# The four expert rows of a token are summed by one strided reduction on VectorE instead of two additions on POOL

## What is computed

```python
topk_idx, topk_weight = _gate(x, gate_w, e_bias)     # 4 of 16 experts for each token
inter = jax.nn.silu(g) * u                            # per expert
expert_out = jnp.einsum('eti,ehi->eth', inter, down_proj)
sel = expert_out[topk_idx, jnp.arange(T)[:, None]]
y = jnp.einsum('tkh,tk->th', sel, topk_weight)        # the sum over the four rows of a token
...
return y + shared_out
...
x = _layernorm(x + _L0_ffn_ref(x, ...), axis=-1)
```

## Time and profile before

| | us |
|---|---|
| median of three runs | 789.55 |
| the three runs | 783.31, 789.55, 789.67 |
| the profiled execution | 784.78 |
| its span (first to last instruction) | 782.1 |

### The profile page before, as it was taken

How to read it: one execution, slowest core, us unless ns; L and a number is a source line. 1 busy time by engine, 2 the same in 40 slices (tenths; PEclk the granted TensorE clock), 3 DMA queues, 4 the chain that set the end, 5 groups by cost and what they waited for, 6 DMA issues and landing times.

```text
span 782.1 us, 24288 instructions
## 1 busy us (share of the span) xinstructions
PE 731.6 (94%) x9544; PEld 508.8 (65%) x9544; DVE 546.0 (70%) x1549; ACT 433.7 (55%) x880; POOL 273.8 (35%) x320
## 2 busy tenths in 40 slices
PE   5979999999999999999999999998799999999983
PEld 2547666756676776567667756776677787775643
DVE  8477755369546686865758599448989558943887
ACT  4867776264756534567565354753146766664331
POOL 7222112011232110625311054230265255556872
PEclk9999999999999999999999999999989999999997
DMA  8335676424000000311300041043686225424461
GB/s 281 141 95 155 189 149 162 126 54 127 2 3 2 3 2 19 120 41 45 95 2 3 2 156 55 9 165 136 210 272 188 64 92 171 147 82 161 141 208 56
DMA packets 55181, 80.78 MB, mean 103 GB/s; under 512 B 12576, under 2 KB 43424, under 8 KB 54560
## 3 DMA queue, kind: packets, MB, share of 16 engines
q1 hardware_dynamic: 48416, 62.71, 26.3%
q0 software_dynamic: 5376, 15.47, 5.1%
q10 hardware_dynamic: 1280, 1.05, 0.5%
HBM read 42.65 MB, written 33.41 MB: 97 GB/s over the span
## 4 chain that ended last, share of the span: by engine, by line
PE 65%; DVE 25%; issue 3%; ACT 2%; DMA 2%; SPq 1%; POOL 1%; ACTq 0%; DVEq 0%
PE ps L1657 28%; PE ps L1663 14%; PE ps L1755 7%; PE ps L1736 3%; PE ps L1880 3%; DVE xmax L1519 3%; PE ps L1771 3%; DVE st L1328 2%; DVE rows L1345 2%; PE ps L1799 1%; PE ps L1772 1%; DVE root_a L1337 1%; SPq L766 1%; PE ps L1944 1%; DVE attn_mem L1485 1%
## 5 line engine op out<-in xcount | busy, mean ns | idle before, releaser
L968 POOL TENSOR_TENSOR qk<-square,qk 128x512 f16<-128x512 f32 x64 | 75.8, 1186 | 258.9 <-ACT qk L1060 258.8
L1657 PE MATMUL ps<-x_split,w_qkv 128*128 128x512 f16 x384 | 93.8, 382 | 2.9 <-DVE qk L1481 1.9
L1663 PEld LDWEIGHTS ps<-attn_mem 128*64 128x64 f32 x1920 | 78.6, 138 | 24.0 <-issue 21.3
L1663 PE MATMUL ps<-attn_mem 128*64 128x65 f32 x1920 | 93.3, 226 | 0.3 <-issue 0.2
L990 POOL DMA_INDIRECT rows_out<-attn_mem,dest x64 | 62.5, 977 | 41.3 <-ACT attn_mem L1161 26.7
L983 POOL DMA_INDIRECT rows_in<-rows,slot_i x48 | 47.5, 989 | 73.3 <-DVE slot_i L1418 61.2
L1481 DVE SCALAR_TENSOR_TENSOR qk<-ps,qk 128x512 f16<-128x512 f32 x64 | 43.8, 684 | 41.8 <-ACT square L1057 41.6
L1063 ACT ACTIVATE attn_mem<-ps 128x512 f32<-128x512 f32 x64 | 37.7, 595 | 62.1 <-PE ps L1736 62.0
L1101 ACT ACTIVATE prob<-ps 128x512 f32<-128x512 f32 x96 | 52.9, 603 | 21.5 <-PE ps L1663 12.2
L1657 PEld LDWEIGHTS ps<-x_split,w_qkv 128*128 128x128 f16 x384 | 37.1, 98 | 37.7 <-issue 3.9
L1657 PE MATMUL ps<-attn_mem,w_qkv 128*128 128x128 f16 x512 | 55.8, 223 | 3.2 <-DVE attn_mem L1585 2.5
(11 more groups left out here) (307 smaller groups left out, 1872.7 us busy)
## 6 DMA issues: line engine op xcount, KB each, us to landing
attn_mem<-rows_in SPq DMA_DIRECT2D x64, 144.0 KB, 2.4
late_mem<-ffn_w SPq DMA_DIRECT2D x17, 384.0 KB, 3.6
rows_in<-zero_row SPq DMA_DIRECT2D x32, 144.0 KB, 4.8
up_split<-late_mem SPq DMA_DIRECT2D x16, 256.0 KB, 2.8
x_stage<-xT SPq DMA_DIRECT2D x4, 512.0 KB, 5.7
down_split<-late_mem SPq DMA_DIRECT2D x16, 128.0 KB, 2.8
rows<-x SPq DMA_DIRECT2D x4, 512.0 KB, 6.9
xq<-late_mem SPq DMA_DIRECT2D x32, 64.0 KB
```

The lines of the kernel that those rows point to most:

```text
L968: pool.tensor_tensor(parts[:, 3, :], square[:, n % 2, :], parts[:, 2, :], ALU.subtract).then_inc(p_sql.sem, 1)
L1657: ins = pe.matmul(dst, lhs(i), rhs(j), start=first and n == 0, stop=last and n == 2)
L1663: ins = pe.matmul(dst[at:at + COLS, :], lhs[:, at:at + COLS], rhs, start=start, stop=stop)
```

## The change

POOL's branch `combine` is removed, and with it the signal `paired`. DVE waits for the landed rows itself, sums the four rows with one `tensor_reduce` whose input is read with the four rows innermost (a stride of 256 floats, 1,024 bytes), into `row_sum`, the first 256 floats of `x_mem`, waits for that by a new signal `joined`, and folds `row_sum` into the sums. The order of all lists, the fetches and the three buffers stay. The sum of the four rows is taken in another order.

```diff
+        row_sum = x_mem[:, 0:D]
...
-        folded = signal("folded"); paired = signal("paired", 2)
+        folded = signal("folded"); joined = signal("joined")
...
-                elif kind == "combine":
-                    i = NT * b + n
-                    four = yg[i % YG]
-                    pool.wait_ge(*yg_loaded[i % YG](i // YG + 1, 0))
-                    pool.tensor_tensor(four[:, 0:2, :], four[:, 0:2, :], four[:, 2:4, :], ALU.add).then_inc(paired.sem, 1)
-                    pool.wait_ge(*paired(i, 1))
-                    pool.tensor_tensor(four[:, 0, :], four[:, 0, :], four[:, 1, :], ALU.add).then_inc(paired.sem, 1)
...
-                    dve.wait_ge(*paired(i + 1, 0))
-                    four = yg[i % YG]
-                    dve.tensor_tensor(total[:, n, :], four[:, 0, :], total[:, n, :], ALU.add).then_inc(folded.sem, 1)
+                    dve.wait_ge(*yg_loaded[i % YG](i // YG + 1, 0))
+                    dve.tensor_reduce(row_sum[:, :], yg[i % YG].rearrange("p k d -> p d k"), AX.X, ALU.add
+                                      ).then_inc(joined.sem, 1)
+                    dve.wait_ge(*joined(i, 1))
+                    dve.tensor_tensor(total[:, n, :], row_sum[:, :], total[:, n, :], ALU.add).then_inc(folded.sem, 1)
                     dve.wait_ge(*folded(0, i + 1))
                     statistics(n, total)
```

## The result

The changed kernel takes **794.89 us** (median of 10 runs, 792.93 to 799.62); the kernel before takes 784.24 (10 runs, 781.27 to 789.67). The ratio of the means is **1.0126, with a 95% interval of 1.0097 to 1.0156**: 9.9 us slower (10.7 between the medians). The forecast was 791, from 3.8 us of loss on a base of 786.8. The base was 2.6 above the median of before, since those runs spread over 8 us and do not sit on two levels, and the loss was too small by a factor of 2.6. The range, 783 to 800, holds the time, but not by the sum: 3.8 on the measured 784.24 would be 788.0. The too high base made up for 2.6 of the missing us, and the upper end of the range was there for rival B. The profiled execution took 792.93, its span is 790.0.

What follows compares the result with a forecast made beforehand. DVE's chain from 733.92 to 771.09 was taken to bound the changed part: reductions add 11.3 us, POOL waits give 5.1 back, some 2 of other waits are filled, so 3.8 more on 786.8 gives 791, range 783 to 800.

Steps and rivals of the forecast that it cites:

- rival B: DVE's new reduction: the stride halves its speed, 2.29 us instead of 1.22, 13 us lost in all; chance 0.22.
- What bounds the stage: From expert 9's gating (733.92) to the first `total` step (771.09), DVE's own chain of 37.17 us sets the time.
- The price of POOL's additions: DVE after 733: of 9.2 us of waits beside POOL, 5.5 belong to `combine`'s two additions and go.
- The reduction at 1.22 us: DVE's new four-row sum: 1024 strided elements take 1.22 us, as a contiguous reduction does, 1.25 with the step.
- nine reductions add 11.3: The nine new reductions on DVE's chain after 733 lengthen it by 11.3 us.
- New collisions: Folds right behind a `dense weigh` meet POOL's `dense keep` and end some 0.6 us late; waits for POOL still about 4.1.
- Rival C: Folds miss POOL's `dense keep`, which falls under the reduction; all 4.1 us of waits go, 0 to -1 us; chance 0.13.
- The stretch before 733 costs 0: Three combines before 733 add 3.8 us to DVE, which fit in its 4.3 us of slack.
- The moved wait: DVE itself waits for fetched rows, landing 3.4 to 7.6 us after issue; 8 us or more are available, so no cost.
- rival D: Fetches land late, so DVE waits for rows once or twice, 1 to 3 us each: 788 to 793; chance 0.05.
- The chances: Whole kernel: 0.03 for faster by over 1%, 0.72 for within 1%, 0.25 for slower by over 1%.

Runs made afterwards that it cites:

- act_order: Changed kernel with ACT's silu of expert 14 put ahead of block 1's `norm3` copies; timed ratio to the kernel before 1.0131.
- contig: Changed kernel with the reduction adding four neighbouring floats, read contiguously (another sum); timed ratio to the kernel before 1.0038.
- nosum: Changed kernel without the sum of four rows, the fold adding row 0 alone; timed ratio to the kernel before 0.9953.
- merge: Kernel before, sums still on POOL, with the inverse roots of blocks 1 and 2 taken as one; timed ratio to it 0.9954.
- tree: Changed kernel with the strided reduction replaced by two contiguous additions on DVE; timed ratio to the kernel before 1.0105.
- poolback: Changed kernel with POOL's two additions put back on scratch data that no result uses; timed ratio to the kernel before 1.0196.
- strides2: Changed kernel with single DVE reductions and additions of several sizes and strides appended at its end; 16 floats took 164 ns contiguous, 179 at 16 bytes.

## Why the prediction was right or wrong

- **What bounds the stage** (DVE's list from gating 9 to the totals): right. act_order moved PE's stop without a change of time; contig, nosum and merge came within 0.3 us of their replays. The replay is too low where more operations meet POOL's: tree came out 1.5 us above it, poolback 2.2.
- **The price of POOL's additions** (5.5 of 9.2 us of waits, and some coming back): right. nosum gives -4.0 for -3.8, poolback shows the waits with nobody waiting for a result.
- **The reduction at 1.22 us: the step that failed.** The term "nine reductions add 11.3" was 9 x 1.97 = 17.7, the 1.93 us with the step behind it. The length itself was read rightly: the row of 1,220 ns was of f16 and had 64 outputs, and contig's reduction of f32 to 256 takes 1.21 as well. What failed was the stride. I took 1.22 since 171 ns for 16 elements at 16 bytes stood beside 170 for 16 contiguous ones. But these were two different reductions, to four outputs and to one. In strides2, where only the stride differs, 16 floats take 164 and 179 ns: the penalty is there, 15 ns, and the comparison was off by 6 already. At 512 floats it is 0.69 against 1.06. A row with 16 elements could not bear a term of 1024.
- **Rival B** (chance 0.22) was the mechanism that came, at 1.63 times per element instead of twice, so 8 to 10 us instead of 13. Its line of decision, a reduction of 1.8 us for a loss of 1%, fits: 1.93 gave 1.26%. Of the prediction's signs of being wrong two came together, a reduction above 1.8 us (B) and all folds at 0.42 (C). The section "Specifications (TRN2)" of the Trainium skill's page "SBUF — State Buffer" says that each crossing to a new 16-byte line pays unless a line is hit twice; the step between 8 and 16 bytes agrees with it. That groups of two pay nothing at 2,048 bytes is not in that sentence.
- **New collisions** (4.1 us of waits left): wrong in the changed kernel, by the same term: at 1.93 the fold comes just as POOL's subtraction ends. In contig they are there, 1.01 for 0.42, six of them for the five forecast. (The working has `dense keep` hold until 2.57; 1.43 + 1.16 is 2.59, which changes nothing.) Rival C had this mechanism; it came about through a longer reduction and not through an earlier subtraction, and so it made the loss smaller but gave no gain.
- **The stretch before 733 costs 0:** wrong by 1.5 us, by the same term again. A combine takes 3.00 us there (723.02 to 726.02) instead of 2.26, and DVE's round for one expert (723.02 to 727.20, 4.18 us) is just above PE's 4.12. So all three rounds from gating 6 to 9 take 4.18, where in the kernel before two took 4.12 and the first only 2.81 (722.87 to 725.68); that short one makes 1.4 of the 1.5. In contig the stretch takes 11.05, as before.
- **The moved wait** for the fetched rows costs nothing: right, no reduction began with a wait for a DMA (rival D falls), and its landing took 3.7 us in the median.
- **The chances** put 0.72 on within 1%; the time came out slower by over 1%, at 0.25. That 791 came within 4 us of 794.89 is in part luck: the base was too high while the loss was too small, and the longer reduction, by missing POOL's subtraction, gave back 3.7 us of its own cost.

## What to carry to other kernels

An operation that an idle engine does for a busy one is not free if the two hold each other up: look for tiny operations with a long maximum in the groups (0.16 us in the median, 1.14 at most), lay the two timelines together, and price the other engine's work by a kernel that leaves it out. Count a strided fp32 pass of VectorE over SBUF at 1.5 to 1.8 times a contiguous one from 16 bytes on (reduction 1.6, addition 1.55 at 16 bytes and 1.8 at 256), and settle such a factor with a row of the size in question, not with one of 16 elements. And where many small steps hang on one list, joining them can give more than a cheaper form of one of them: here one root for two blocks gave 4.9 us, and leaving out the sums altogether 4.0.

## What the runs showed that was not expected

- The strided penalty has its edge between 8 and 16 bytes, in the reduction hardly depends on the distance (1.86 to 1.97 us from 16 to 1,024 bytes), and is absent where the pass alternates between two places (1.24 and 0.43 us).
- DVE and POOL hold each other up in both directions: POOL's subtraction takes 1.16 us alone and 1.33 to 1.47 when it comes second, DVE's fold 0.42 and 1.26. Steps of four elements with one input in SBUF are hit as well (L1331, 0.17 and 1.00), the reduction, `bn_stats` (0.43) and the passes that read PSUM (0.68) are not.
- A faster operation can cost part of its gain by its end alone: 0.71 us less in each of nine reductions shortened the chain by 2.7 us and not by 6.4, as its follower then met POOL.
